# New places for about forty instructions in the 72-step attention period of a transformer block

## The reference

```python
q, k, v = rope(h @ Wq), rope(h @ Wk), h @ Wv     # h: layer norm of x, modulated; 32 query heads, 8 key/value heads
scores = q @ k.T / sqrt(64), causal mask          # 2 sequences of 1024 tokens, head width 64
out = softmax(scores) @ v                         # four query heads share one key/value head
x = x + ga * (out @ Wo)
```

## Time and profile before

| what | value |
|---|---|
| time, median of 3 runs | 1797.01 us (1793.49 to 1798.22) |
| the profiled execution's own time | 1796.64 us |
| its span, first to last instruction | 1794.9 us |
| mean granted TensorE clock | 0.992 |
| busy over the span: PE, DVE, ACT, POOL | 1724.8, 1237.0, 1140.9, 976.9 us |
| warm-up and prologue, until head 0 starts | 81.6 us |
| period of heads 0 to 6 | 143.7 to 145.0 us each |
| head 7 with the run-out | 154.7 us |
| output projection and feed-forward | from 1245 us on |

### The profile page before, as it was taken

How to read it: one execution, slowest core, us unless ns; L and a number is a source line. 1 busy time by engine, 2 the same in 40 slices (tenths; PEclk the granted TensorE clock), 3 DMA queues, 4 the chain that set the end, 5 groups by cost and what they waited for, 6 DMA issues and landing times. The chain is left out here.

```text
span 1794.9 us, 28096 instructions
## 1 busy us (share of the span) xinstructions
PE 1724.8 (96%) x9505; PEld 1388.3 (77%) x9505; DVE 1237.0 (69%) x2006; ACT 1140.9 (64%) x2315; POOL 976.9 (54%) x821
## 2 busy tenths in 40 slices
PE   7899999999999999999999999988999899999998
PEld 3587887887787878788778778767788688888886
DVE  6788888888888888788888888884233454535333
ACT  5687787787787878778778778893233453323221
POOL 1266767767666676676676767635100044444453
PEclk9999999999999999999999999999999899999999
DMA  7343444444344354354344434555555300101000
GB/s 284 80 116 91 127 115 118 111 114 125 87 129 120 96 139 112 86 136 111 102 124 113 124 105 119 133 156 162 175 188 187 106 1 1 53 1 53 1 30 24
DMA packets 174969, 190.95 MB, mean 106 GB/s; under 512 B 31456, under 2 KB 117736, under 8 KB 174832
## 3 DMA queue, kind: packets, MB, share of 16 engines
q1 hardware_dynamic: 137840, 140.99, 27.7%
q10 hardware_dynamic: 36992, 48.25, 9.7%
HBM read 86.12 MB, written 31.74 MB: 66 GB/s over the span
## 5 line engine op out<-in xcount | busy, mean ns | idle before, releaser
L1086 DVE TENSOR_TENSOR p_lo<-ps_b,p_hi 128x512 fp32r<-128x512 f32 x576 | 395.6, 687 | 158.7 <-ACT p_hi L971 154.1
L986 ACT ACTIVATE p<-ps_b,negm 128x640 f32<-128x640 f32 (+7 forms) x512 | 382.1, 749 | 119.8 <-DVE negm L1094 115.7
L971 ACT CAST p_hi<-ps_b 128x512 fp32r<-128x512 f32 x576 | 337.0, 588 | 103.2 <-PE ps_b L871 82.3
L1094 DVE TENSOR_REDUCE negm<-ps_b 128x1 f32<-128x640 f32 (+7 forms) x512 | 376.5, 745 | 31.0 <-PE ps_b L861 28.8
L871 PE MATMUL ps_b<-ident,p 128*128 128x128 f32 x2304 | 349.8, 275 | 7.4 <-DVE p_lo L1086 6.3
L854 PE MATMUL ps_b<-k_hh,q_hl 128*128 128x512 f32 (+3 forms) x768 | 268.6, 350 | 28.7 <-ACT p L986 27.5
L871 PEld LDWEIGHTS ps_b<-ident,p 128*128 128x128 f32 x2304 | 252.4, 141 | 35.0 <-DVE p_lo L1086 9.5
L885 PE MATMUL ps_b<-p_hi,v_hl 128*128 128x512 f32 x576 | 263.2, 457 | 1.9 <-ACT o_sb L979 1.4
L855 PE MATMUL ps_b<-k_l,q_hl 128*128 128x512 f32 (+3 forms) x768 | 255.7, 345 | 0.0
L886 PE MATMUL ps_b<-p_lo,v_hl 128*128 128x512 f32 x576 | 227.7, 395 | 0.0
L1721 PE MATMUL ps_d<-h_hi,gu 128*128 128x512 f32 x512 | 201.4, 393 | 1.6 <-DVE h_lo L1841 1.6
(11 more groups left out here) (160 smaller groups left out, 3178.4 us busy)
## 6 DMA issues: line engine op xcount, KB each, us to landing
rot_x<-rot_s SPq DMA_DIRECT2D x320, 64.0 KB, 2.0
q_hl<-rot_s SPq DMA_DIRECT2D x128, 128.0 KB, 2.4
q_hl<-rot_x SPq DMA_DIRECT2D x128, 128.0 KB, 2.4
rd_all<-reciprocals SPq DMA_DIRECT2D x128, 128.0 KB, 3.1
o_low<-o_sb ACTq DMA_DIRECT2D x128, 128.0 KB, 2.4
attention_out<-o_sb SPq DMA_DIRECT2D x128, 128.0 KB, 2.6
o_raw<-attention_out SPq DMA_DIRECT2D x32, 512.0 KB, 4.9
wf<-in_L_ffn_w_gate_up ACTq DMA_DIRECT2D x28, 256.0 KB, 3.1
```

What stands on the lines that cost most here:

```text
L971: act.copy(p_hi[:, T % P_RING, :], ps[:, T_BANK + T % 2, :]).then_inc(phi_ready, 1)
L986: act.activation(p_32[:, parity, h, column * P:column * P + nk], s, ACT.Exp, bias=negm[:, k:k + 1], scale=1.0, accum_out=den[:, parity, k: ...
L1086: dve.tensor_tensor(p_lo[:, T % P_RING, :], ps[:, T_BANK + T % 2, :], p_hi[:, T % P_RING, :].bitcast(F32), ALU.subtract).then_inc(plo_read ...
L1094: dve.tensor_reduce(negm[:, k:k + 1], s, AX.X, ALU.max, negate=True).then_inc(max_ready, 1)
```

## The change

Only tables of places change; the same instructions are issued, with the same operands and the same waits, in another order on TensorE, ScalarE, VectorE and GpSimd. The order on SP and the warm-up's tables stay.

```diff
 TURNS = Places(own_tiles(0), 100, {
-    11: (10, 303), 19: (18, 511), 20: (19, 511), 25: (24, 511), 35: (34, 511), 39: (38, 301), 66: (65, 101),
-    71: (70, 511)})
+    8: (7, 201), 35: (34, 511), 43: (42, 201), 71: (70, 511)})
 VALUES = Places(own_tiles(LAG), 200, {
-    0: (2, 900), 2: (4, 511), 3: (4, 512), 8: (10, 301), 9: (11, 900), 16: (18, 900), 18: (20, 900), 23: (24, 512),
-    24: (26, 900), 27: (29, 900), 32: (34, 900), 36: (38, 900), 44: (46, 501), 45: (47, 900), 52: (54, 900),
+    0: (2, 900), 1: (4, 101), 2: (5, 101), 8: (10, 900), 9: (11, 900), 16: (18, 101), 18: (20, 900), 24: (26, 900),
+    26: (28, 511), 27: (29, 900), 32: (34, 900), 36: (38, 900), 44: (46, 501), 45: (47, 900), 52: (54, 900),
...
 PROJECTIONS = Places(own_pieces(), 300, {
-    (0, 0): (1, 101), (0, 2): (4, 101), (2, 0): (9, 800), (3, 0): (14, 101), (3, 1): (14, 102), (4, 0): (19, 800),
-    (4, 2): (22, 101), (5, 0): (24, 800), (5, 1): (27, 101), (5, 2): (27, 102), (6, 0): (31, 201), (7, 0): (36, 501),
-    (7, 3): (38, 901), (9, 0): (44, 800), (10, 0): (49, 501), (11, 0): (54, 800), (12, 0): (59, 501), (12, 1): (61, 201),
-    (12, 2): (62, 101), (13, 0): (67, 501), (13, 2): (69, 301)}, early=PROJECTIONS_EARLY)
+    (0, 0): (1, 101), (2, 0): (9, 800), (3, 0): (14, 101), (3, 1): (14, 102), (4, 0): (19, 800), (5, 0): (24, 201),
+    (5, 2): (27, 101), (6, 0): (31, 201), (7, 0): (36, 501), (7, 1): (38, 101), (9, 0): (44, 800), (10, 0): (49, 501),
+    (10, 2): (52, 101), (11, 0): (54, 800), (12, 0): (59, 501), (12, 1): (61, 201), (12, 2): (62, 101),
+    (13, 0): (67, 101)}, early=PROJECTIONS_EARLY)
 VALUE_TURNS: 1: (6, 501) -> (6, 511)
 SCORES: 22: (24, 520) -> (24, 501)
 MASKS: 8: (10, 302) out, 9: (11, 101) in; 38: (42, 530) -> (43, 501)
-KEY_SCALES = Places({0: W_SCALE}, 100)
+KEY_SCALES = Places({0: W_SCALE}, 100, {
+    0: (27, 201)})
+VALUE_HIGHS: 8: (42, 201)
+HIGHS: 11: (10, 311), 30: (29, 201), 40: (39, 601), 66: (65, 201)
+KEY_HIGHS: 13: (75, 601)
+UNIT_SIGNS: 3: (43, 201)
+MAXIMA: 3: (4, 301), 25: (28, 201), 27: (31, 301), 50: (57, 301)
+LOWS: 55: (55, 511)
+RECIPROCAL_TURNS: 3: (29, 701)
+UNIT_SUMS: 0: (4, 201), 3: (41, 301)
+WEIGHT_LOWS: 2: (31, 302)
+HALF_SUMS: 5: (29, 111), 10: (53, 401)
+ROTARY_SUMS: 5: (28, 101)
+UNIT_SCALES: 5: (62, 311)
```

More of the change, by code:

```diff
@@ L435 @@
 VALUES = Places(own_tiles(LAG), 200, {
[2 rows of a table removed]
[2 rows of a table added]
     54: (56, 900), 55: (58, 101), 60: (62, 900), 63: (65, 900), 68: (70, 900)})
 PROJECTIONS = Places(own_pieces(), 300, {
[3 rows of a table removed]
-    (12, 2): (62, 101), (13, 0): (67, 501), (13, 2): (69, 301)}, early=PROJECTIONS_EARLY)
[3 rows of a table added]
+    (13, 0): (67, 101)}, early=PROJECTIONS_EARLY)
 VALUE_TURNS = Places(own_uses(("v",), 0), 400, {
-    1: (6, 501), 8: (41, 201)})
+    1: (6, 511), 8: (41, 201)})
 SCORES = Places(own_rows(0), 500, {
-    6: (6, 520), 14: (15, 501), 22: (24, 520), 30: (33, 520), 38: (42, 520), 46: (51, 501), 54: (60, 501), 62: (69, 520)}, early=SCORES_EARLY)
+    6: (6, 520), 14: (15, 501), 22: (24, 501), 30: (33, 520), 38: (42, 520), 46: (51, 501), 54: (60, 501), 62: (69, 520)}, early=SCORES_EARLY)
 MASKS = Places(own_rows(0), 510, {
-    6: (6, 530), 8: (10, 302), 14: (15, 530), 22: (24, 530), 30: (33, 530), 38: (42, 530), 46: (51, 530), 54: (60, 530),
+    6: (6, 530), 9: (11, 101), 14: (15, 530), 22: (24, 530), 30: (33, 530), 38: (43, 501), 46: (51, 530), 54: (60, 530),
     62: (69, 530)}, early=MASKS_EARLY)
-KEY_SCALES = Places({0: W_SCALE}, 100)
+KEY_SCALES = Places({0: W_SCALE}, 100, {
+    0: (27, 201)})
 ROUNDINGS = Places({0: W_HIGH}, 110)
 VALUE_ROWS = Places(own_uses(("kv",), 4), 120)
-VALUE_HIGHS = Places(own_uses(("v",), 1), 130)
-HIGHS = Places(own_tiles(0), 200)
+VALUE_HIGHS = Places(own_uses(("v",), 1), 130, {
+    8: (42, 201)})
+HIGHS = Places(own_tiles(0), 200, {
+    11: (10, 311), 30: (29, 201), 40: (39, 601), 66: (65, 201)})
 COPIES = Places(own_blocks(LAG), 300)
@@ L459 @@
     6: (7, 420), 14: (16, 420), 22: (25, 420), 30: (34, 420), 38: (43, 420), 46: (52, 420), 54: (61, 420), 62: (70, 420)}, early=EXPONENTIALS_EARLY)
-KEY_HIGHS = Places(own_uses(("kv",), 8), 500, early=in_warm_up(("kv",), KEYS_AT))
+KEY_HIGHS = Places(own_uses(("kv",), 8), 500, {
+    13: (75, 601)}, early=in_warm_up(("kv",), KEYS_AT))
 QUERY_HIGHS = Places(own_uses(("qx", "qy"), 8), 510, early=in_warm_up(("qy",), QUERIES_AT))
 UNIT_ABS = Places(own_units(3), 600)
-UNIT_SIGNS = Places(own_units(3), 610)
+UNIT_SIGNS = Places(own_units(3), 610, {
+    3: (43, 201)})
 UNIT_STORES = Places(own_units(15), 620)
@@ L468 @@
 MAXIMA = Places(own_rows(1), 200, {
-    6: (7, 220), 14: (16, 220), 22: (25, 220), 30: (34, 220), 38: (43, 220), 46: (52, 220), 54: (61, 220), 62: (70, 220)}, early=MAXIMA_EARLY)
-LOWS = Places(own_tiles(0), 300)
+    3: (4, 301), 6: (7, 220), 14: (16, 220), 22: (25, 220), 25: (28, 201), 27: (31, 301), 30: (34, 220), 38: (43, 220),
+    46: (52, 220), 50: (57, 301), 54: (61, 220), 62: (70, 220)}, early=MAXIMA_EARLY)
+LOWS = Places(own_tiles(0), 300, {
+    55: (55, 511)})
 RECIPROCALS = Places(own_pairs(0), 400)
-RECIPROCAL_TURNS = Places(own_pairs(1), 410)
-UNIT_SUMS = Places(own_units(4), 500)
+RECIPROCAL_TURNS = Places(own_pairs(1), 410, {
+    3: (29, 701)})
+UNIT_SUMS = Places(own_units(4), 500, {
+    0: (4, 201), 3: (41, 301)})
 UNIT_PICKS = Places(own_units(7), 510)
-WEIGHT_LOWS = Places({k: W_LOW + k for k in range(CT)}, 700)
-HALF_SUMS = Places(own_blocks(LAG + 3), 100)
+WEIGHT_LOWS = Places({k: W_LOW + k for k in range(CT)}, 700, {
+    2: (31, 302)})
+HALF_SUMS = Places(own_blocks(LAG + 3), 100, {
+    5: (29, 111), 10: (53, 401)})
 DIVISIONS = Places(own_blocks(LAG + 4), 110)
-ROTARY_SUMS = Places(own_uses(("kv", "qx", "qy"), 6), 200)
+ROTARY_SUMS = Places(own_uses(("kv", "qx", "qy"), 6), 200, {
+    5: (28, 101)})
 KEY_LOWS = Places(own_uses(("kv",), 8), 300, early=in_warm_up(("kv",), KEYS_AT))
 QUERY_LOWS = Places(own_uses(("qx", "qy"), 8), 310, early=in_warm_up(("qy",), QUERIES_AT))
-UNIT_SCALES = Places(own_units(5), 400)
+UNIT_SCALES = Places(own_units(5), 400, {
+    5: (62, 311)})
 UNIT_HATS = Places(own_units(8), 410)
```

## The result

The changed kernel took 1777.54 us, the median of four runs (1777.29 to 1777.76), beside 1795.58 us for the kernel before on the same chip: a ratio of 0.9894, 95% interval 0.9878 to 0.9911. The forecast was 1775 us.

A forecast was written before the change was run, and what follows sets the result against it. TensorE's work plus its waits bound heads 0 to 6; -0.12 + 0 + 1.2 + 0.9 + 0.6 + 0.5 = 3.1 us a period, times seven 22 us, off the 1797.01 us median: about 1775 us, range 1767 to 1792.

The forecast's parts named there:

- steps 24 to 33: Scores 28 and 30 stop waiting, less a new 0.75 us wait at turn 30: 1.2 us a period, 0.1 to 1.4.
- 51 to 59: Maximum 50 goes ahead of the rotaries, so the wait of scores 52 goes: 0.6 us a period, 0.3 to 0.65.
- steps 37 to 45: Maximum 35 starts earlier, so the wait of scores 38 goes: 0.9 us a period, 0.4 to 1.1.
- 62 to 70: High 66 goes ahead of exponentials 57, so the wait of scores 60 goes: 0.5 us a period, 0.2 to 0.5.
- What bounds it: In heads 0 to 6, TensorE's own work plus its waits; waits for exponentials together 4.07 us a period.
- TensorE's own work: More wide matmuls behind narrow ones, 11 instead of 9 a period: 0.12 us lost, 0 to 0.2.
- the tie: Weight low 0 (VectorE) or rotary sum 5 (GpSimd) first on the shared port: 0.15 us decides over 1 us.
- rival 1: Rotary sum 5 starts before weight low 0, scores 28 still waits: 14 us won in all, 1783 us; chance 0.27.
- case (a): Weight low 0 starts before rotary sum 5; waits of scores 28 and 30 both go: 1.34 us a period won.
- Head 7: Projects nothing for a next head; moves help and hurt: 0 taken, -2 to +4 us the ends.
- Rivals 2 and 3: 2: new waits return half or more of 4.07 us, chance 0.16; 3: late swap delays copy 6, slower, chance 0.12.

The follow-up runs named there:

- e10: e8 with TensorE's order of steps 0 to 23 as in the kernel before; 1769.25 us.
- e6: The kernel before with only the change's part of steps 37 to 45; 1788.62 us.
- e7: The kernel before with only maximum 50 ahead of rotaries 11 and high 66 ahead of exponentials 57; 1789.23 us.
- e11: The changed kernel with weight low 0 alone moved to right behind low 28, ahead of rotary sum 5; 1777.37 us.
- e8: The changed kernel with low 55, rotary sum 5, half sum 5 put back, weight lows 0 to 3, unit sum 2, unit scale 2 moved; 1768.41 us.

## Why the prediction was right, and where it wasn't

The sum came out (3.02 us a period for 3.1), not each term. About 0.7 us that was forecast and did not come (steps 24 to 33 and 51 to 59) was met by about 0.6 that came unforecast (steps 37 to 45 and 62 to 70): that the sum is within 0.1 is partly luck. Measured by the starts of turns in the two traces, mean of the seven periods:

- **What bounds it**: right. The period lost what TensorE had waited; its busy time moved by 0.6 of the 3.3 us. One reading of the list of waits was wrong: the 40 waits are not five in each of eight periods, but two in the warm-up (4.2 and 0.6 us), 34 in heads 0 to 6 (four to six each) and four in head 7. The sum of 4.07 us came from one period's rows and doesn't rest on that.
- **TensorE's own work**: 0.12 us forecast; 0.11 to 0.16 us are lost between steps 3 and 12 and 0.11 between 18 and 24 (heads 1 to 6; head 0 won 0.49 us between steps 3 and 12). e10 shows the second as own work, the first has a wait under it in the old order.
- **Steps 24 to 33**: 1.2 us forecast, 0.88 measured. The step that failed is the tie: "it waits for its swap transfer, so it starts at about 574.05 as before". Rotary sum 5 did wait for its swap: in all seven periods of each of the fourteen traces it starts 0.07 us behind the landing of the last of the four swap transfers. But the swap did not land as before. Before, the shift of copy 5, a transfer on ScalarE's queue, was issued 0.06 us behind that last swap transfer on SP; SP's issue, ScalarE's, then the swap's issue-to-landing time:

```profile
571.42 0.59 SPq L723 DMA_DIRECT2D rot_x<-rot_s  x1
571.48 0.48 ACTq L944 DMA_DIRECT2D o_low<-o_sb  x1
rot_x<-rot_s SPq DMA_DIRECT2D x1, 64.0 KB, 2.6
```

  The change put high 30 (step 29, place 201) ahead of the shift (place 310) on ScalarE, and the shift comes 1.73 us behind the swap transfer:

```profile
564.35 0.59 SPq L735 DMA_DIRECT2D rot_x<-rot_s  x1
566.08 0.47 ACTq L956 DMA_DIRECT2D o_low<-o_sb  x1
rot_x<-rot_s SPq DMA_DIRECT2D x1, 64.0 KB, 2.0
```

  So the swap took 2.04 us instead of 2.55, and rotary sum 5 started 60.21 us into the head instead of 60.62. Head 4 of the kernel before had shown the same: there the shift came 0.55 us behind the swap transfer, the swap took 1.97 us, and rotary sum 5 started at 60.04. In the 21 periods of the kernel before, e6 and e7, which have the old order here, the shift came 0.13 us or more behind in four; in those four weight low 0 took 1.06 to 1.62 us, in the other 17 0.54 or 0.55. No run moved the shift alone, so that it is the cause rests on these traces. With weight low 0 at 60.58 (forecast 573.9, or 60.47) the tie was lost by 0.4 us: rival 1's condition came true. But rival 1 was priced at 0.15 us net from the same wrong start: maximum 26 worked out at 577.4, 63.97 us into the head, began at 63.40. So 0.89 of the 1.45 us at scores 28 went even so, with all of scores 30, and the time fell where the forecast had put the other case. And the 1.2 us of case (a) was not there to be had in this order (e11).
- **Steps 37 to 45**: 0.9 forecast, 1.22 measured in six heads (1.17 alone in e6), a term too small; head 4, with the waits that only the execution before had there, brings the mean to 1.42. The chain went as written; what I left out is turn 45. The rows of projection (9, 0) and turn 45 before:

```profile
603.29 0.39 PE L820 MATMUL ps_b<-hT_lo,w_hi 128*128 128x512 f32 x1
603.80 0.63 PE L871 MATMUL ps_b<-ident,p 128*128 128x128 f32 x4
```

  and after:

```profile
594.42 0.39 PE L832 MATMUL ps_b<-hT_lo,w_hi 128*128 128x512 f32 x1
594.65 0.60 PE L883 MATMUL ps_b<-ident,p 128*128 128x128 f32 x4
```

  0.51 us apart before, 0.23 after: 0.28 us without a bracket, which the list of waits doesn't show. Low 43, earlier now, is what turn 45 needs: before, turn 45 starts 0.15 us behind the end of low 43 in every head, in the changed kernel 0.44 us behind it.
- **Steps 51 to 59**: 0.6 forecast and 0.60 measured between 58 and 60, but turn 57 took 0.40 back. The step that failed: "Low 55 and rotary sum 10 come later, both with over 1 us to spare." I put pick 4 at its old 0.65 us and didn't ask what half sum 10, moved in the same edit, would do beside it.
- **Steps 62 to 70**: 0.5 forecast, 0.6 measured.
- **Head 7**: 0 forecast, 0.1 us longer to the end in these two executions. Its attention did get shorter, by 1.8 us up to the output projection's first matmul; what stands behind, where no order was changed, took as much longer this time. Over all the runs the time from the start of head 7 to the end lies between 700.0 and 705.7 us, so the term is not told apart from nothing.
- **Rivals 2 and 3**: new waits did take back 0.66 + 0.40 us a period, a quarter of what went, not half. Values 32 never waited for copy 6: copy 6 began 68.47 us into the head, before at 69.64.

ScalarE of the changed kernel, high 28, exponentials 26 and copy 6, for the earlier trace rows:

```profile
563.33 0.64 ACT L983 CAST p_hi<-ps_b 128x512 fp32r<-128x512 f32 x1
...
570.90 1.12 ACT L998 ACTIVATE p<-ps_b,negm 128x1024 f32<-128x1024 f32 x1 [2.35 <-DVE negm L1106]
...
574.72 0.59 ACT L991 COPY o_sb<-ps_b 128x512 f32<-128x512 f32 x1
```

High 28 is at 57.08 us into the head, forecast 57.07 (570.5).

## What to carry to other kernels

Before an operation is moved on GpSimd or VectorE, list what stands beside it on the other of the two, at its new time and at that of everything behind it: each move here that cut one meeting made another, until the weight lows were spread so that little was left of the meetings (0.55 to 0.84 us each in e8). A wait for a transfer isn't a fixed time either: compare its issue-to-landing time with that of other periods, and ask what the change does to transfers issued close to it on another queue (here a moved cast took a shift away from a swap, and a tie of 0.15 us fell the other way). And compare starts in two traces step by step; the 0.28 us of turn 45, a tenth of the gain, had no bracket.

## What the runs showed of the hardware

The Trainium skill, page "SBUF — State Buffer", section "SBUF: two separate sides", says that the one of the two that starts first has the shared port pair for the whole instruction. The runs agree: a weight low of 0.55 us lasted until 0.42 us behind the end of the GpSimd operation that it met, a pick of 0.65 us until 0.55 us behind it. Three things I had not expected. A GpSimd operation is recorded from where it starts, and held up it only looks longer: division 4 took 1.61 us instead of 1.27 beside weight low 0. When a second GpSimd operation followed at once, a waiting weight low got in ahead of it in each of the 103 such meetings in the fourteen traces. A waiting pick did so in some heads and not in others: in the changed kernel pick 4 took 1.62 and 1.60 us in heads 1 and 5, with rotary sum 10 drawn out to 1.74, but 2.81 to 2.87 us, both operations first, in heads 0, 4 and 6. The same instructions went both ways, so neither their kind nor the bf16 operands decide it alone; what does stays open. And the last of the swap transfers (64 KB on SP's queue) took 1.97 to 2.04 us to land in 81 of the 98 periods, but 2.30 to 2.99 us in the 17 in which the shift (128 KB on ScalarE's queue) was issued between 0.42 us ahead of it and 0.10 us behind it.
